# Two heads instead of four in the body of an attention loop

## What is computed

```python
def attention(x, adj, Wq, Wk, Wv, Wo):          # layer 1; n = 3327 tokens, d = 128, h = 8
    q = (x @ Wq.T).reshape(d, n, h)             # 128 "heads" d, each with 8 features
    k = (x @ Wk.T).reshape(d, n, h)
    v = (x @ Wv.T).reshape(d, n, h)
    a = jnp.einsum('dnh,dmh->dnm', q, k) * scale
    a = a + adj + adj
    a = jax.nn.softmax(a, axis=2)
    out = jnp.einsum('dnm,dmh->dnh', a, v)
    return out.reshape(n, h * d) @ Wo.T

h = jnp.maximum(_layernorm(x), 0.0)             # layer 0, before it
x = x + (adj / rowsum(adj)) @ h @ W_in + (adj.T / rowsum(adj.T)) @ h @ W_out
h = jnp.maximum(_layernorm(x), 0.0)
x = x + attention(h, adj, Wq, Wk, Wv, Wo)
```

## Time and profile before

| | us |
|---|---|
| median of 3 runs | 11,779.06 |
| lowest and highest run | 11,767.22 and 11,779.27 |
| the profiled execution: its time | 11,756.2 |
| the profiled execution: span from first to last instruction | 11,754.5 |
| attention stage in it (with L1019 to L1096) | about 820 to 11,640 |

### The profile page before, as it was taken

How to read it: one execution, slowest core, us unless ns; L and a number is a source line. 1 busy time by engine, 2 the same in 40 slices (tenths; PEclk the granted TensorE clock), 3 DMA queues, 4 the chain that set the end, 5 groups by cost and what they waited for, 6 DMA issues and landing times. The chain is left out here.

```text
span 11754.5 us, 545122 instructions
## 1 busy us (share of the span) xinstructions
PE 10907.4 (93%) x216535; PEld 6944.7 (59%) x216535; DVE 10367.8 (88%) x10893; ACT 10429.1 (89%) x9224; POOL 6442.3 (55%) x3236
## 2 busy tenths in 40 slices
PE   8759999999999999999999999999999999999998
PEld 6525556555656556565655666656565566656566
DVE  7778988898988989888988898989888898988897
ACT  3359999999999999999999999999999999999996
POOL 4345555555555555555555555555555555555554
PEclk9889999999999999999999999999999999999999
DMA  6571111111121111111112111111112111111112
GB/s 223 179 232 39 39 39 39 39 39 39 39 69 44 39 39 39 39 39 38 40 39 75 39 39 39 39 39 39 39 36 77 39 39 37 40 38 38 39 39 81
DMA packets 573045, 653.23 MB, mean 56 GB/s; under 512 B 172173, under 2 KB 511251, under 8 KB 566867
## 3 DMA queue, kind: packets, MB, share of 16 engines
q1 hardware_dynamic: 570130, 617.66, 19.0%
q0 software_dynamic: 832, 1.71, 0.0%
HBM read 485.17 MB, written 133.77 MB: 53 GB/s over the span
## 5 line engine op out<-in xcount | busy, mean ns | idle before, releaser
L1074 DVE SCALAR_TENSOR_TENSOR at_double<-attention_adj_t,at_score 128x832 f32<-128x832 f32 x10240 | 9698.2, 1016 | 1127.8 <-PE at_score L1019 1121.9
L999 POOL TENSOR_TENSOR at_single<-at_single,attention_adj_t 128x832 f32<-128x832 f32 x3072 | 6106.0, 1988 | 4728.3 <-ACT at_single L1088 4695.6
L1091 ACT ACTIVATE at_double<-at_double 128x1664 f32<-128x1664 f32 x5120 | 8100.9, 1633 | 108.0 <-DVE at_double L1074 99.4
L1019 PE MATMUL at_score<-at_q,at_k 128*32 128x512 bf16 (+1 forms) x106496 | 7538.8, 353 | 450.8 <-ACT at_double L1091 383.9
L1035 PE MATMUL at_acc<-at_double,at_v 128*9 128x208 f32 x81920 | 5694.0, 344 | 151.2 <-issue 150.3
L1019 PEld LDWEIGHTS at_score<-at_q,at_k 128*32 128x32 bf16 x106496 | 3730.0, 145 | 2856.1 <-DVE at_double L1074 1126.9
L1088 ACT ACTIVATE at_single<-at_score 128x832 f32<-128x832 f32 x3072 | 2760.9, 899 | 657.9 <-PE at_score L1019 657.6
L1035 PEld LDWEIGHTS at_acc<-at_double,at_v 128*9 128x9 f32 x81920 | 2213.9, 92 | 1236.8 <-issue 255.0
L1035 PE MATMUL at_acc<-at_single,at_v 128*9 128x208 f32 x24576 | 1677.2, 341 | 0.0
L1035 PEld LDWEIGHTS at_acc<-at_single,at_v 128*9 128x9 f32 x24576 | 667.6, 92 | 292.3
L287 POOL TENSOR_TENSOR layer_col_acc<-layer_col_acc,st_a_rows 128x3328 f32<-128x3328 f32 x26 | 189.2, 7276 | 181.2 <-DMA st_a_rows<-in_adj_dram 181.2
(11 more groups left out here) (123 smaller groups left out, 1251.9 us busy)
## 6 DMA issues: line engine op xcount, KB each, us to landing
at_k<-k_parts_scratch SPq DMA_DIRECT2D x1536, 156.0 KB
at_q<-q_parts_scratch SPq DMA_DIRECT2D x4608, 13.0 KB
at_v<-v_scratch SPq DMA_DIRECT2D x512, 112.5 KB
adj_t_scratch<-st_a_t SPq DMA_DIRECT2D x26, 1664.0 KB, 7.6
st_a_rows<-in_adj_dram SPq DMA_DIRECT2D x25, 1663.5 KB, 8.8
attention_adj_t<-adj_t_scratch SPq DMA_DIRECT2D x16, 2080.0 KB, 16.5
attended_scratch<-at_o SPq DMA_DIRECT2D x1920, 7.3 KB
q_parts_scratch<-pr_partsq SPq DMA_DIRECT2D x39, 512.0 KB, 4.6
```

What stands on the lines that cost most here:

```text
L999: pool.tensor_tensor(slot(n), slot(n), at[:, plan.chunk[n], :], ALU.mult).then_inc(multiplied, 1)
L1019: last = pe.matmul(score[plan.buffer(n)][32 * t:32 * (t + 1), a:b], keys[:, 32 * t:32 * (t + 1)], q[k][:, a:b], start=True, stop=True, til ...
L1074: dve.scalar_tensor_tensor(out=slot(n), in0=at[:, plan.chunk[n], :], scalar=2.0, in1=score[plan.buffer(n)][:, 0:NB], op0=ALU.mult, op1=ALU ...
L1091: act.activation(doubles[buffer][:], doubles[buffer][:], ACT.Exp).then_inc(exped, 1)
```

## The change

```diff
-GROUP = 4
+GROUP = 2
...
     def buffer(self, n):
 
-        return n % self.n % SCORES
+        n %= self.n
+        return n % SCORES if self.n % SCORES != 1 or n < self.n - 1 else 1
```

## The result

| | before | after |
|---|---|---|
| median of the runs, us | 11,773.1 (4 runs, 11,721.6 to 11,779.3) | 12,647.5 (4 runs, 12,642.8 to 12,658.1) |
| ratio, 95% interval | | 1.075 (1.072 to 1.079) |
| span of the profiled execution, us | 11,754.5 | 12,648.0 |
| attention body | 4 heads, 84.5 us | 2 heads, 45.7 us |

The change makes the kernel 7.5% slower: not the forecast case but rival 2, whose sum was 12,664.

A forecast was written before the change was run, and what follows sets the result against it. ScalarE was taken to bound the attention stage, idling 747 us at TensorE's loop-backs. Removing 747 and adding 255 x (3.0 + 0.5) = 893 gave +146: 11,756 + 146 + 23 = 11,925 us, range 11,100 to 12,700.

The forecast's parts named there:

- the forecast case: TensorE's attention loop-backs: one miss each, 255 x (3.0 + 0.5) us replacing 747 us, 11,925 us in all; chance 40%.
- rival 2: TensorE's attention loop: all instructions fetched anew each turn, 255 x 6.4 = 1,632 us, 12,664 us in all; chance 27%.
- 127 at 5.9 us: Attention stage before the change: ScalarE's 747 us idle are 127 loop-backs of the attention body, 5.9 us each.
- The count of loop-backs and blocks: TensorE's shorter attention body: 255 loop-backs instead of 127, 1,754 instructions in 8 blocks, a ninth fetched ahead.
- I take it that the body is kept except for the first block: TensorE's loop-back: the block fetched ahead takes only the first one's place, one miss and a 3.31 us gap each.
- +146 us: Whole kernel: net change forecast, 747 us gone and 255 x (3.0 + 0.5) = 893 us added.
- The price of a single gap, 3.0 us: ScalarE's idle time per TensorE loop-back with one miss: 4.76 minus 1.72 us, taken as 3.0, bounds 2.5 to 4.2.
- The score buffers: End of each body: three buffers do not divide 52 steps, delaying ScalarE 0.5 us per body, 0.6 at most.
- The wait of step 51: Step 51 reuses the score buffer of step 49 and waits for its exponential, its sum starting 0.6 us late.
- the second short distance: Another score buffer reused two steps earlier, waiting for a sum instead of an exponential; put at zero.
- Five double buffers and the other engines' loops at zero: Attention stage: five double buffers instead of eight cost zero; other engines looping twice as often cost zero, 0.2 us at most.
- Rival 1: TensorE's attention loop: the whole body is kept, 747 us go and 128 come, 11,160 us in all; chance 28%.

The follow-up runs named there:

- runs at 11,200 and 12,324 us: Changed kernel with 224 or 344 always-met waits ahead of TensorE's attention loop, putting its last 8 or 68 instructions in an eighth block: 11,200 and 12,324 us.
- the run with one gap: Changed kernel with 344 always-met waits ahead of TensorE's attention loop, so 68 of its instructions lie in an eighth block: 12,324 us.
- the loop in seven blocks: Changed kernel with 168 always-met waits (84 instructions) ahead of TensorE's attention loop, moving its start: 11,180 us, ratio 0.949.
- the two kernels with the exception at step 8 and refetching: Changed kernel with the score-buffer order's exception at step 8 instead of 51: 12,357 us; the same with TensorE looping every two bodies: 11,780 us.

## Why the forecast missed

- **What bounds the kernel, and why it idles there: right.** ScalarE sets the pace and its idle time belongs to TensorE's refetched loop-backs. 127 at 5.9 us was the reading; removing 64 of them gave 371 us, 5.8 each.
- **The count of loop-backs and blocks: right.** 255 loop-backs, eight blocks and a ninth fetched ahead. The runs at 11,200 and 12,324 us place the end of a block within some 60 instructions of where the working had it.
- **"I take it that the body is kept except for the first block": wrong, and this is the step that failed.** I chose among three ways in which a ninth block can displace another, without a row that told them apart: it displaces none, the first alone, or one after another. I took the middle one. The runs show that one block too many costs nine packets per body, all of the loop and the one ahead, and each loop-back has its first gap and most have both. That turned +146 us into the measured +874.
- **The price of a single gap, 3.0 us: wrong too, 4.5 us measured.** I subtracted the second gap from a loop-back without slow clock and let the slow clock come in half of them at most. In the run with one gap the clock is at 0.51 after each of the two loop-backs shown and after some 250 of the 255. Had my mechanism been right, the answer would still have been some 380 us too low: 255 x 1.5.
- **The score buffers: place right, size low.** 0.5 us forecast, 0.8 to 0.85 measured; how much of it belongs to each of the two waits is inferred. The wait of step 51 was right (0.64 us of TensorE's time, 0.6 worked out); the second short distance behind it was taken as free because the same distance at steps 0 and 1 of the old body seemed free. It was not: the heads with it last 19.8 us in the kernel before, not 19.5 (5043.68 in the earlier trace rows less 5023.88, the end of the head before it, in the same timeline of ScalarE):

```profile
5023.88 0.39 ACT L1096 ACTIVATE at_o<-at_acc 128x208 f32<-128x208 f32 x1
```

- **Five double buffers and the other engines' loops at zero: right.** The first by a run of its own, the second by the loop in seven blocks: 255 loop-backs of ScalarE and 256 of VectorE, and heads of 19.51 us where neither a fetch nor a short distance falls into one.
- **Rival 2's sum, 12,664: right to 0.13%.** Its two terms (5.9 and 0.5) are 5.75 and 0.8 in the runs, so they err in opposite directions, and that the sum comes this close is in part luck.
- **Rival 1 is real, one shift away.** Its sum was 11,160; the loop in seven blocks took 11,180. What decided was not whether the fetch ahead displaces a block (it does) but how many blocks the loop touches.

The Trainium skill's "Runtime: NRT & Kernel Launch", section "Instruction fetch mechanics", has 2,048 instructions for TensorE, which is eight blocks of 256; the runs at 11,180 and 12,324 us agree with eight, the fetched-ahead one included. Its 2-page window does not hold for TensorE here: 1,754 instructions in seven blocks stay for 255 turns. The prediction's own evidence against that window, VectorE's 232 instructions, was weak: no row says which engine's instructions q14 carries.

## What to carry to other kernels

Look for a loop whose instructions are fetched in every turn: packets on the instruction queue that never pause, and once per body an idle gap that no semaphore explains. Count the blocks that the loop touches, not its instructions, add the one fetched ahead, and if it is one too many, shorten the loop or move its start by some instructions that run once: here that was worth 12% of the changed kernel and 5% against the kernel before. If it cannot fit, write more turns into one: a refetch costs the same for 3,500 instructions as for 7,000. A gap on an engine that is not the bound may still cost the bound more than its length.

## What the runs showed of the hardware

- TensorE's instruction blocks are 16.4 KB; the loop of 1,754 instructions stays while it touches seven and is fetched whole, nine packets per turn, when it touches eight with 68 instructions in the last. With 8 in the last, one fetch ahead is followed by eight more, nine packets in all, and the next turn has none.
- The kernel whose loop-backs fetch nothing has a granted clock of 1.00 over the stage; one gap of 2.9 us per body was followed by 0.51 for the next 3.4 us at some 250 of 255 loop-backs.
- The block fetched ahead is not fetched when the loop-back follows 8 instructions after a block's start (by the working of where blocks begin), but for two turns in 255.
- The first gap is labelled in the waits with an exponential of ScalarE that ended long before; a gap of that size with the same label at each loop-back was the fetch. In the two kernels with the exception at step 8 and refetching, the same gap is labelled "issue", as in the waits of the changed kernel with that exception:

```profile
PE at_score L1020 <- issue: 741.4, 254, 5.4
```
